# A vision-tower layer on one core: ScalarE clears the hidden-value tile, token weights arrive in three parts, and all five engines run their calls in another order

## The chip, the cores and the metric

The program runs on one core of a Trainium2 chip. The metric is the device time of one execution in microseconds (us). The profile is one further execution, recorded by the hardware profiler. Engine names: PE is TensorE (PEld its weight loads), DVE VectorE, ACT ScalarE, POOL GpSimd, SP SyncE, which here only issues DMAs.

## What is computed

```python
def reference(x, ...):                       # x: 32 images, 3 x 96 x 96, float32
    p = patches(x)                           # 32 x 36 tokens of 768 values
    h = layernorm(layernorm(p, ln1) @ W_tok, ln2)          # tokens of 192 values
    q, k, v = split(h @ W_qkv)               # 8 heads of 24 channels
    q, k = q / norm(q, tokens), k / norm(k, tokens)
    a = softmax(einsum('bnhd,bnhe->bhde', q, k) * temp)    # channel by channel, per image
    h = layernorm(h + (a applied to v) @ W_proj + b_proj)
    xn, sp = l2(h), l2(slots) * scale        # 8 experts of 4 slots
    logits = xn @ sp
    D, C = softmax(logits, experts), softmax(logits, all slots)
    H = gelu(down(einsum(xn, D)) + b_down)   # 24 hidden values per slot
    return layernorm(h + einsum(up(H) + b_up, C))
```

## The kernel before, in words

The 1152 tokens are handled in two cuts. For the token embedding there are 9 tiles `t` of 128 tokens; from attention on there are 11 groups `g` of up to 3 images, 108 tokens each (the last has 72). Everything is float32, and PE runs each float32 product as two matmul records.

Each engine runs its own list of calls, written out in the kernel; a call issues one to some dozens of instructions, and starts when semaphores say that its inputs are there and its output buffer is free. Each engine takes its list strictly in that order. So the order of the lists is the whole schedule.

Start: SP loads `gb1` (gain and offset of the first norm), the token weights `wt` (6 blocks of 128 x 192, in two DMAs), and the tokens twice, `xT` turned for the products and `xs` plain for the statistics. `first_products` (L449) multiplies a constant tile `still` 6 times, with a result that nobody reads. `column_means` and `offset` (L454, L464) multiply the weights by gain shares and by offsets; DVE makes the centred weights `wc` of them; `token(t)` (L473) is the embedding.

Per tile: `x_stats`, `x_moments` (DVE), `ln1_var`, `ln1_root` (POOL), `token_out` (DVE, reads the product), `token_stats`, `token_moments` (DVE), `ln2_var`, `ln2_root` (POOL), `ln2_norm` (DVE), `turn_h` (PE), `take_h` (ACT). `token(t)` may overwrite its PSUM bank only after `token_out(t-2)`. `keep_h_gain` and `keep_h_offset` (POOL) keep the normalised tokens for the residual. They need three rows that `load_rows` fetches and broadcasts to 128 partitions (`g2row`, `b2row`, `bprow`, one semaphore `rows_in` for all three). `regroup(g)` (SP) copies them to the layout by groups.

Per group, attention: `qkv` (PE), `square`, `take_qk`, `take_v`, `square_k` (ACT), `norms` and `gram` (PE), `norm_logs`, `norm_roots` (ACT), `q_scale` (POOL), `scales`, `scores`, `score_max`, `score_shift` (DVE), `exp_e` (ACT), `turn_p` (DVE), `mix` (PE), `y_sums`, `y_norm` (DVE), `project` (PE), `residual` and the norm after it. `qkv(g+1)` may overwrite only after `square(g)`, `take_qk(g)` and `take_v(g)`. `take_qk(0)` needs the small constant `imgsel`.

Per group, slots: `unit_h1` (DVE), `turn_xn`, `logits` (PE), `mask_logits` (DVE), `turn_l` (PE), the two softmaxes (`max_c`, `max_d`, `exp_c`, `exp_d`, `invert_sums`, `scale_d`), `turn_dc` and `slot_in` (PE). The experts run in two halves, groups 0 to 7 and 8 to 10: `hidden(b)` (PE), `gelu(b)` (ACT, after a table load), `spread(b)` (DVE) into `hb`, whose other places must be zero. Then per group `slot_out` (PE), `slot_bias` (DVE), `combine` (PE), `last_residual`, `last_stats`, `last_moments` (DVE), `ln4_root` (POOL), `last_shift` (DVE), `last_norm` (ACT) and `store` (SP). For the last group DVE ends it with `last_out`.

POOL clears tiles at the start; the last and largest is `hb`, L1202.

Of the kernel before, what the change touches and what calls it, by code (L numbers as in the profile page):

```python
# [74 lines left out]
def build(nc, x, x_t, w_tok, ln1_gb, ln2_g, ln2_b, g2col, b2col, w_qk, w_v, w_rest, w_proj, b_proj, temp, slots, scale,  # L75
# [3 lines left out]
    with ctx:  # L79
# [180 lines left out]
        wtok_in = [sem(f"wtok_in{i}") for i in range(2)]  # L260
# [187 lines left out]
        def _(pe):  # L448
            def first_products():  # L449
                pe.wait_ge(still_ready, 1)  # L450
                for _ in range(6):
                    pe.matmul(ps[:, 2, 0:D], still[:, 0:128], still[:, :], start=True, stop=True)

            def column_means():  # L454
                pe.wait_ge(gs1_ready, 1)
                for kc in range(KC):
                    if kc % (KC // 2) == 0:
                        pe.wait_ge(wtok_in[kc // (KC // 2)], 16)
# [4 lines left out]
            def offset():  # L463
                pe.wait_ge(ln1_in, 16)  # L464
                pe.wait_ge(wtok_in[0], 16)
                pe.wait_ge(wtok_in[1], 16)
# [218 lines left out]
            norms(5); turn_h(8); project(3); qkv(7); mix(4); norms(6); gram(5); turn_xn(0); project(4)
            logits(0); qkv(8); mix(5); norms(7); gram(6); turn_l(0); turn_xn(1); project(5); qkv(9)
            mix(6); gram(7); norms(8); logits(1); turn_dc(0); turn_xn(2); project(6); turn_l(1)
            norms(9); gram(8); qkv(10); gram(9); logits(2); turn_xn(3); mix(7); turn_l(2); slot_in(0)
            turn_xn(4); norms(10); logits(3); project(7); turn_dc(1); turn_l(3); logits(4); turn_xn(5)
# [662 lines left out]
```

## Time and profile before

| | us |
|---|---|
| median of 3 runs (112.24 to 112.75) | 112.63 |
| the profiled execution | 112.18 |
| its span, first to last instruction | 110.4 |

The profile's page gives, for the span of 110.4 us, each engine's busy time, the busy share in 40 slices, the chain of work that ended last, and groups of instructions. A PE that is busy throughout a stretch has no hole there; the ends of matmuls are modelled, so that does not say it works at its peak. The granted clock of the span is 0.991. A `[0.30 <-DVE h L757]` behind a row is the idle time of that engine before the instruction and what ended it.

### The profile page before, as it was taken

To read this page: it belongs to the slowest core of one execution; us is meant where nothing else is said; L and a number is where in the kernel's file an instruction comes from. 1 tells how busy PE (TensorE), PEld (TensorE's weight loads), DVE (VectorE), ACT (ScalarE), POOL (GpSimd) and SP (SyncE) were. 2 spreads that over 40 slices of the span, in tenths; PEclk is the share of its full clock that TensorE was granted. 3 is DMA by queue.
4 is the path that set the end of the run, shared out by engine and by line. 5 is a ranking of instruction groups with operands and counts; after the bars stand their busy time and mean duration, and the time that the engine had idled before them with its cause. 6 is when DMAs were issued, how large, how long until landed. Compare 5 with 4: busy or idle time off the path is not lost. (4 is left out here: it accounts for less than half of the span.)

```text
span 110.4 us, 4479 instructions
## 1 busy us (share of the span) xinstructions
PE 101.7 (92%) x1607; PEld 88.2 (80%) x1607; DVE 87.7 (79%) x380; ACT 67.5 (61%) x222; POOL 53.4 (48%) x126
## 2 busy tenths in 40 slices
PE   6999999999999999999999999799989989999900
PEld 6999989979999887887898887679779668879500
DVE  2129756968998958958977989999999897999960
ACT  4000023729563887798887996787785994476570
POOL 8800552263999887847204417906030340076880
PEclk9999999999999999999999999999999999999996
DMA  2999999469501111111000000010042000002232
GB/s 23 334 339 394 389 386 398 153 212 342 235 0 30 36 32 40 29 35 32 6 3 6 0 6 0 6 48 24 30 105 72 7 0 3 0 6 84 66 112 58
DMA packets 8554, 11.27 MB, mean 102 GB/s; under 512 B 2358, under 2 KB 5878, under 8 KB 8534
## 3 DMA queue, kind: packets, MB, share of 16 engines
q1 hardware_dynamic: 8533, 11.00, 29.5%
q8 instruction: 13, 0.21, 0.8%
q14 instruction: 8, 0.06, 0.2%
HBM read 9.22 MB, written 0.88 MB: 92 GB/s over the span
## 5 line engine op out<-in xcount | busy, mean ns | idle before, releaser
L480 PE MATMUL ps<-wc,xT 128*128 128x192 f32 x108 | 19.1, 330 | 0.0
L480 PEld LDWEIGHTS ps<-wc,xT 128*128 128x128 f32 x108 | 17.4, 190 | 0.7 <-issue 0.6
L1046 ACT ACTIVATE hT<-ps,b,g 128x128 f32<-128x128 f32 x18 | 7.3, 463 | 16.4 <-PE ps L491 16.3
L1068 ACT ACTIVATE km<-ps,imgsel 108x192 f32<-108x192 f32 (+1 forms) x32 | 11.1, 420 | 3.7 <-PE ps L515 3.6
L1256 POOL TENSOR_SCALAR mv<-mv 108x1 f32<-108x1 f32 (+1 forms) x11 | 3.0, 270 | 14.4 <-DVE mv L856 14.4
L568 PE MATMUL ps<-wp,yT 128*108 128x192 f32 (+1 forms) x44 | 9.3, 333 | 0.0
L664 PE MATMUL ps<-wu,hb 128*96 128x192 f32 (+1 forms) x44 | 9.2, 332 | 0.1
L1261 POOL TENSOR_TENSOR r<-mv,halves 108x2 f32<-108x2 f32 (+1 forms) x11 | 8.8, 803 | 0.8
L508 PE MATMUL ps<-wqk,hT 128*108 128x192 f32 (+1 forms) x44 | 9.0, 326 | 0.0
L726 DVE BATCH_NORM_STATS2 st<-xs 128x6 f32<-128x384 f32 x18 | 8.9, 537 | 0.0
L1249 POOL TENSOR_TENSOR rqt<-rn,tempc 128x6 f32<-128x6 f32 x11 | 2.2, 199 | 12.1 <-ACT rn L1105 12.1
L1207 POOL TENSOR_SCALAR var<-mv 128x1 f32<-128x1 f32 x9 | 2.0, 219 | 11.8 <-DVE mv L731 11.5
L1078 ACT ACTIVATE sqk<-km 108x576 f32<-108x576 f32 (+1 forms) x11 | 7.5, 683 | 0.0
L664 PEld LDWEIGHTS ps<-wu,hb 128*96 128x96 f32 (+1 forms) x44 | 6.5, 161 | 0.8 <-issue 0.4
L593 PE MATMUL ps<-sp,xnT 96*108 96x96 f32 (+1 forms) x44 | 6.2, 264 | 0.7 <-ACT xnT L1111 0.4
L568 PEld LDWEIGHTS ps<-wp,yT 128*108 128x108 f32 (+1 forms) x44 | 6.4, 170 | 0.5 <-DVE yT L836 0.2
L559 PE MATMUL ps<-vT,pc 32*32 32x37 f32 x512 | 6.8, 195 | 0.0
L1162 ACT ACTIVATE o<-z,sh,rstd 108x192 f32<-108x192 f32 x10 | 5.1, 543 | 2.8 <-DVE sh L980 2.8
L1269 POOL TENSOR_TENSOR rstd<-var,mhalf 108x1 f32<-108x1 f32 (+1 forms) x11 | 6.3, 576 | 0.9
L506 PE MATMUL ps<-hT,wv 128*128 128x108 f32 (+1 forms) x44 | 6.6, 273 | 0.0
L559 PEld LDWEIGHTS ps<-vT,pc 32*32 32x32 f32 x512 | 5.5, 104 | 1.3
L508 PEld LDWEIGHTS ps<-wqk,hT 128*108 128x108 f32 (+1 forms) x44 | 6.4, 171 | 0.0
(118 smaller groups left out, 296.6 us busy)
## 6 DMA issues: line engine op xcount, KB each, us to landing
xT<-in_x_t SPq DMA_DIRECT2D x9, 384.0 KB, 6.4
xs<-in_x SPq DMA_DIRECT2D x9, 384.0 KB, 6.2
out<-o SPq DMA_DIRECT2D x10, 81.0 KB
wt<-in_w_tok SPq DMA_DIRECT2D x2, 288.0 KB, 3.2
wqk<-in_w_qk SPq DMA_DIRECT2D x1, 192.0 KB, 5.9
wp<-in_w_proj SPq DMA_DIRECT2D x1, 192.0 KB, 10.0
wd<-in_w_down SPq DMA_DIRECT2D x1, 192.0 KB
z<-h SPq DMA_DIRECT2D x2, 81.0 KB
```

Source lines behind the costliest of these rows:

```text
L480: mm = pe.matmul(tokp(t), xT[:, o + kc * 128:o + (kc + 1) * 128], wc[:, kc, :], start=kc == 0, stop=kc == KC - 1)
L506: pe.matmul(vp(g)[:, m, :], wv[:, m, :], main, start=True, stop=False)
L508: pe.matmul(qkp(g)[:, m, :], main, wqk[:, m * D:(m + 1) * D], start=False, stop=False)
L559: mm = pe.matmul(yp(g)[r, m, i, :], pc[r, g % 2, GI * m + i, :], vT[r, m, g * GI + i, :], start=True, stop=True, tile_position=(32 * j, 32 ...
L568: mm = pe.matmul(prp(g), yT[:, g % NY, m, 0:images(g), :].rearrange("p i n -> p (i n)"), wp[:, m, :], start=m == 0, stop=m == 1)
L664: mm = pe.matmul(ytp(g), hb[:, e, i0:i0 + ni, :, :].rearrange("p i n q -> p (i n q)"), wu[:, e, :], start=e == 0, stop=e == 1)
L726: ins = dve.bn_stats(st1[:, t % 2, h, :], xs[:, t % NB, h * (PD // 2):(h + 1) * (PD // 2)])
L1046: ins = act.activation(hT[:, f, t * 128:(t + 1) * 128], htp(t)[:, f, :], ACT.Identity, bias=b2[:, f:f + 1], scale=g2[:, f:f + 1])
L1068: act.activation(km[0:n, g % NK, i, :], qkp(g)[:, 1, :], ACT.Copy, scale=imgsel[0:n, i:i + 1])
L1078: act.activation(sqk[0:n, g % 2, 0:ni, :], km[0:n, g % NK, 0:ni, :], ACT.Square).then_inc(sqk_ready, 1)
L1261: pool.tensor_tensor(r3[0:n, g, :], mv3[0:n, g, 1:3], halves[0:n, :], ALU.pow).then_inc(r3_ready, 1)
L1269: pool.tensor_tensor(rstd4[0:n, g:g + 1], var4[0:n, g:g + 1], mhalf[0:n, 0:1], ALU.pow).then_inc(rstd4_ready, 1)
```

## The change

`hb` is no longer cleared by POOL but by one ScalarE instruction, `clear_hidden`, with a semaphore of its own that only `spread(0)` waits for; the five clears that stay are counted with `cleared`, 5. The token weights come in `WP = 3` DMAs of two blocks each. `first_products` makes 5 products. All lists are written anew.

```diff
+WP = 3
-        wtok_in = [sem(f"wtok_in{i}") for i in range(2)]
+        wtok_in = [sem(f"wtok_in{i}") for i in range(WP)]
+        hb_cleared = sem("hb_cleared")
-                k0 = i * KC // 2
-                sp.dma_start(wt[:, k0:k0 + KC // 2, :].rearrange("p k e -> p (k e)"),
-                             w_tok[:, k0 * D:(k0 + KC // 2) * D]).then_inc(wtok_in[i], 16)
+                k0 = i * KC // WP
+                sp.dma_start(wt[:, k0:k0 + KC // WP, :].rearrange("p k e -> p (k e)"),
+                             w_tok[:, k0 * D:(k0 + KC // WP) * D]).then_inc(wtok_in[i], 16)
-                for _ in range(6):
+                for _ in range(5):
                     pe.matmul(ps[:, 2, 0:D], still[:, 0:128], still[:, :], start=True, stop=True)
-                    if kc % (KC // 2) == 0:
-                        pe.wait_ge(wtok_in[kc // (KC // 2)], 16)
+                    if kc % (KC // WP) == 0:
+                        pe.wait_ge(wtok_in[kc // (KC // WP)], 16)
-                    dve.wait_ge(cleared, 6)
+                    dve.wait_ge(hb_cleared, 1)
+            def clear_hidden():
+                act.wait_ge(still_ready, 1)
+                act.activation(hb[:, :, :, :, :].rearrange("p e i n q -> p (e i n q)"),
+                               still[:, 0:1].broadcast_to([128, 2 * B * NE * NP]), ACT.Copy,
+                               scale=0.0).then_inc(hb_cleared, 1)
-            take_h(0); take_h(1); square(0); take_qk(0); take_v(0); square_k(0); square(1); norm_logs(0)
+            take_h(0); take_h(1); square(0); take_qk(0); take_v(0); take_h(2); square_k(0); take_v(1)
+            take_qk(1); square(1); norm_logs(0); square_k(1); norm_roots(0); clear_hidden(); take_qk(2)
-            pool.memset(hb[:, :, :, :, :], 0.0).then_inc(cleared, 1)
-            pool.wait_ge(cleared, 6)
+            pool.wait_ge(cleared, 5)
-            ln2_root(1); ln1_var(2); ln1_root(2); ln2_var(2); ln1_var(3); ln2_root(2); ln1_root(3)
+            ln2_root(1); ln1_var(2); ln1_root(2); ln2_var(2); ln2_root(2); keep_h_gain(0); row_sum()
...
```

The new lists hold the same calls as the old ones, plus `load_token_weights(2)` and `clear_hidden()`.

SP, the DMAs of the first microseconds, with `load_rows` as `g2row`, `b2row`, `bprow`. Before:

```order
L395 DMA wrest<-in_w_rest 128x320
L375 DMA xT<-in_x_t 128x768
L390 DMA imgsel<-const_imgsel 128x3
L380 DMA xs<-in_x 128x768 x2
L375 DMA xT<-in_x_t 128x768 x2
L380 DMA xs<-in_x 128x768
L402 DMA g2row<-in_ln_g 128x192
L403 DMA b2row<-in_ln_b 128x192
L404 DMA bprow<-in_b_proj 128x192
L398 DMA tempc<-in_temp 128x2
```

and now:

```order
L397 DMA wrest<-in_w_rest 128x320
L377 DMA xT<-in_x_t 128x768
L404 DMA g2row<-in_ln_g 128x192
L405 DMA b2row<-in_ln_b 128x192
L406 DMA bprow<-in_b_proj 128x192
L392 DMA imgsel<-const_imgsel 128x3
L382 DMA xs<-in_x 128x768 x2
L409 DMA negmask<-const_negmask 128x96
```

The three rows have moved ahead of two `xT` and three `xs` tiles, and `imgsel` from in front of them to behind them.

POOL, after the root of the second norm of tile 1 (`mhalf` is the exponent of the root; `var1`, `rstd1` belong to the first norm, `var2`, `rstd2` to the second). Before:

```order
L1207 TENSOR_SCALAR var1<-mv1 128x1
L1211 TENSOR_TENSOR rstd1<-var1,mhalf 128x1
L1215 TENSOR_SCALAR var2<-mv2 128x1
L1207 TENSOR_SCALAR var1<-mv1 128x1
L1219 TENSOR_TENSOR rstd2<-var2,mhalf 128x1
L1211 TENSOR_TENSOR rstd1<-var1,mhalf 128x1
L1207 TENSOR_SCALAR var1<-mv1 128x1
L1211 TENSOR_TENSOR rstd1<-var1,mhalf 128x1
```

and now:

```order
L1214 TENSOR_SCALAR var1<-mv1 128x1
L1218 TENSOR_TENSOR rstd1<-var1,mhalf 128x1
L1222 TENSOR_SCALAR var2<-mv2 128x1
L1226 TENSOR_TENSOR rstd2<-var2,mhalf 128x1
L1233 TENSOR_TENSOR h0<-h0,g2row 128x192
L1243 TENSOR_TENSOR b2row<-b2row,bprow 128x192
L1233 TENSOR_TENSOR h0<-h0,g2row 128x192
L1214 TENSOR_SCALAR var1<-mv1 128x1
L1218 TENSOR_TENSOR rstd1<-var1,mhalf 128x1
```

`keep_h_gain(0)`, `row_sum` and `keep_h_gain(1)` now stand ahead of `ln1_var(3)`; before they stood behind `ln1_var(5)`.

PE, around `qkv(10)` (the first four lines of `hT,wv` to `hT,wrest`, 72 tokens) and `mix(7)` (`vT,pc`); `ident,lm` is `turn_l`, `sp3,xnT` is `logits`, `ident,xn` is `turn_xn`. Before:

```order
L515 MATMUL ps<-hT,wrest 128x72 x2
L545 MATMUL ps<-km,qp 32x72 x8
L593 MATMUL ps<-sp3,xnT 108x96 x2
L579 MATMUL ps<-ident,xn 96x108 x2
L559 MATMUL ps<-vT,pc 32x37 x24
L606 MATMUL ps<-ident,lm 96x108
L634 MATMUL ps<-dm,xn 96x96 x2
L579 MATMUL ps<-ident,xn 96x108 x2
```

and now:

```order
L595 MATMUL ps<-sp3,xnT 108x96 x2
L532 MATMUL ps<-imgsel,sq 32x3 x8
L536 MATMUL ps<-sqk,ones 32x144 x4
L547 MATMUL ps<-km,qp 32x72 x8
L608 MATMUL ps<-ident,lm 96x108
L508 MATMUL ps<-hT,wv 128x72 x2
L510 MATMUL ps<-wqk,hT 72x192 x2
L513 MATMUL ps<-wrest,hT 72x192 x2
L517 MATMUL ps<-hT,wrest 128x72 x2
L561 MATMUL ps<-vT,pc 32x37 x24
```

`logits(2)` and `turn_l(2)`, with more work between them, have moved ahead of `qkv(10)`; `mix(7)` still follows it.

## Rows read from the trace of the kernel before

**Rows 1.** The page: busy us, share, instructions; PE's busy tenths in 40 slices.

```profile
PE 101.7 (92%) x1607; PEld 88.2 (80%) x1607; DVE 87.7 (79%) x380; ACT 67.5 (61%) x222; POOL 53.4 (48%) x126
...
PE   6999999999999999999999999799989989999900
```

**Rows 2.** Stretches: us, each engine's busy (instructions), granted PE clock, DMA share, GB/s.

```profile
70.00:75.00 5.00, 4.19 (x100) 3.42 (x98) 5.00 (x27) 3.97 (x19) 1.89 (x4) 1.00 0.12 33
...
85.00:90.00 5.00, 4.36 (x87) 3.14 (x86) 4.59 (x22) 4.38 (x11) 1.75 (x4) 1.00 0.06 14
...
95.00:100.00 5.00, 4.68 (x61) 3.76 (x60) 4.75 (x25) 2.92 (x8) 2.79 (x8) 1.00 0.01 3
```

**Rows 3.** Timeline, PE, PEld and POOL at the start: start us, us, instruction, [idle before].

```profile
1.10 4.21 PE L452 MATMUL ps<-still 128*128 128x192 f32 x12 [1.10 <-DVE still L704]
3.17 1.85 POOL L1202 MEMSET hb<- 128x2048 f32 x1
5.10 2.54 PE L459 MATMUL ps<-wt,gs 128*128 128x192 f32 x12
7.48 2.11 PE L468 MATMUL ps<-wt,gb 128*128 128x192 f32 x12
11.33 0.22 POOL L1207 TENSOR_SCALAR var<-mv 128x1 f32<-128x1 f32 x1 [6.30 <-DVE mv L731]
15.45 0.20 PEld L491 LDWEIGHTS ps<-ident,h 128*128 128x128 f32 x2 [0.30 <-DVE h L757]
```

**Rows 4.** DMA issues: count, KB each, median us from issue to landing.

```profile
wt<-in_w_tok SPq DMA_DIRECT2D x2, 288.0 KB, 3.2
...
bprow<-in_b_proj SPq DMA_DIRECT2D x1, 96.0 KB, 10.4
...
tempc<-in_temp SPq DMA_DIRECT2D x1, 1.0 KB, 9.3
```

**Rows 5.** Timeline of SP's queue: issues behind which the constants land.

```profile
1.19 0.88 SPq L370 DMA_DIRECT2D wt<-in_w_tok  x2
...
13.46 0.43 SPq L404 DMA_DIRECT2D bprow<-in_b_proj  x1
13.94 0.43 SPq L398 DMA_DIRECT2D tempc<-in_temp  x1
```

**Rows 6.** Stretches as in rows 2, while the rows are fetched.

```profile
16.00:18.00 2.00, 2.00 (x16) 1.98 (x14) 1.52 (x4) 0.73 (x2) 0.44 (x1) 1.00 1.03 402
20.00:21.00 1.00, 1.00 (x7) 1.00 (x8) 1.00 (x4) 1.00 (x4) 0.00 (x0) 1.00 0.28 98
```

**Rows 7.** Timelines of PE, ACT and POOL, 18 to 28 us.

```profile
21.91 0.59 PE L506 MATMUL ps<-hT,wv 128*128 128x108 f32 x4
24.55 2.22 PE L480 MATMUL ps<-wc,xT 128*128 128x192 f32 x12
20.13 1.04 ACT L1068 ACTIVATE km<-ps,imgsel 108x192 f32<-108x192 f32 x3
21.25 0.38 ACT L1085 ACTIVATE vT<-ps 128x216 f32<-128x216 f32 x1
18.65 0.57 POOL L1211 TENSOR_TENSOR rstd<-var,mhalf 128x1 f32<-128x1 f32 x1
27.74 0.59 POOL L1236 TENSOR_TENSOR b2row<-b2row,bprow 128x192 f32<-128x192 f32 x1
```

**Rows 8.** ACT groups by shape: count, busy us, mean ns.

```profile
L1078 ACT ACTIVATE sqk<-km 108x576 f32<-108x576 f32 x10 | 7.0, 699 | 0.0
...
L1057 ACT ACTIVATE sq<-ps 108x192 f32<-108x192 f32 x10 | 3.4, 342 | 3.7 <-PE ps L515 3.7
```

**Rows 9.** Timeline: the longest hole on PE after the start.

```profile
71.47 0.30 PE L606 MATMUL ps<-ident,lm 108*96 108x108 f32 x1 [0.59 <-DVE lm L890]
```

**Rows 10.** Timelines of PE and DVE near the end.

```profile
99.58 0.58 PE L677 MATMUL ps<-yt,cT 96*108 96x192 f32 x2 [0.32 <-DVE yt L948]
107.39 0.37 DVE L974 TENSOR_SCALAR o<-z,mv,rstd 72x192 f32<-72x192 f32 x1 [0.69 <-POOL rstd L1269]
```

More of the change, by code:

```diff
@@ L464, in offset @@
                 pe.wait_ge(ln1_in, 16)
[L465 to L466 removed]
+                for i in range(WP):
+                    pe.wait_ge(wtok_in[i], 16)
                 for kc in range(KC):
@@ L685, in _ @@
[L685 to L689, printed above, removed]
@@ L690, in _ @@
-            mix(8); slot_in(1); turn_xn(6); turn_l(4); logits(5); turn_dc(2); project(8); turn_l(5)
-            logits(6); slot_in(2); gram(10); turn_l(6); turn_dc(3); turn_xn(7); mix(9); turn_dc(4)
+            token(3); turn_h(1); qkv(0); token(4); turn_h(2); qkv(1); norms(0); gram(0); token(5)
+            qkv(2); norms(1); turn_h(3); token(6); turn_h(4); qkv(3); norms(2); gram(1); mix(0)
+            token(7); project(0); turn_h(5); qkv(4); norms(3); gram(2); mix(1); token(8); project(1)
+            turn_h(6); qkv(5); mix(2); norms(4); gram(3); turn_h(7); project(2); qkv(6); mix(3)
@@ new lines, in _ @@
+            norms(5); gram(4); turn_h(8); project(3); qkv(7); mix(4); norms(6); gram(5); turn_xn(0)
+            project(4); logits(0); qkv(8); mix(5); gram(6); norms(7); turn_l(0); turn_xn(1); project(5)
+            qkv(9); gram(7); mix(6); logits(1); norms(8); gram(8); turn_l(1); turn_xn(2); project(6)
+            turn_xn(3); turn_dc(0); logits(2); norms(9); gram(9); turn_l(2); qkv(10); mix(7); turn_xn(4)
+            logits(3); slot_in(0); project(7); turn_l(3); turn_xn(5); turn_dc(1); logits(4); norms(10)
@@ new lines, in _ @@
+            take_qk(1); square(1); norm_logs(0); square_k(1); norm_roots(0); clear_hidden(); take_qk(2)
+            take_v(2); take_h(3); norm_logs(1); square(2); square_k(2); norm_roots(1); exp_e(0)
+            take_qk(3); norm_logs(2); norm_roots(2); take_v(3); take_h(4); square_k(3); square(3)
+            exp_e(1); square(4); take_qk(4); norm_logs(3); norm_roots(3); square_k(4); take_v(4)
+            take_h(5); exp_e(2); take_h(6); square(5); take_qk(5); take_v(5); square_k(5); take_h(7)
@@ new lines, in _ @@
+            norm_logs(4); exp_e(3); norm_roots(4); take_qk(6); take_v(6); square(6); norm_logs(5)
+            norm_roots(5); square_k(6); exp_e(4); take_h(8); square(7); take_v(7); take_qk(7)
+            take_xn(0); norm_logs(6); square_k(7); exp_e(5); norm_roots(6); take_qk(8); take_v(8)
+            square(8); exp_c(0); norm_logs(7); exp_d(0); square_k(8); take_xn(1); exp_e(6)
+            norm_roots(7); take_qk(9); take_v(9); square_k(9); norm_logs(8); norm_roots(8); take_xn(2)
+            exp_d(1); square(9); exp_c(1); take_c(0); exp_e(7); norm_logs(9); norm_roots(9); exp_e(8)
@@ new lines, in _ @@
+            exp_d(2); exp_c(2); take_xn(3); take_v(10); square(10); take_qk(10); take_xn(4)
+            take_slots(0); square_k(10); take_xn(5); exp_d(3); take_c(1); exp_e(9); exp_c(3); exp_c(4)
+            take_slots(1); take_xn(6); exp_d(4); take_c(2); norm_logs(10); norm_roots(10); exp_c(5)
+            take_slots(2); exp_d(5); take_xn(7); take_c(3); exp_c(6); exp_d(6); take_c(4); take_slots(3)
+            take_c(5); take_slots(4); exp_c(7); exp_d(7); take_c(6); take_slots(5); take_xn(8)
```

188 lines of the change are left out of this document (85 added, 103 removed).

## Prediction

> **What bounds the kernel now.** I read the page's busy line first [rows 1]. PE is busy for 101.7 of 110.4 us, DVE for 87.7. So PE is the first candidate, and the question is where it has holes. The slices say that from its first product to slice 25, 69 us, it is full [rows 1]. The stretches of 5 us give the size of the holes behind that [rows 2]: 0.81 us in 70 to 75, 0.64 in 85 to 90, 0.32 in 95 to 100. In 70 to 75 DVE is busy for all 5.00 us, and the longest hole ends with the masked logits that DVE writes [rows 9]. So there are three parts. Up to 70 us PE's work sets the time and an order can only lose, unless it takes work off PE. From 70 to 100 us PE and DVE alternate. After 105 us a short chain runs over POOL's roots to DVE's last instruction at 107.39 [rows 10]. The holes in these stretches sum to 1.77 us, which is about all that a new order alone can win on PE; removed work comes on top.
>
> **The constant product.** The 6 products take 4.21 us [rows 3], 0.70 each by their busy time. The 6 products of `offset`, of the same shape, take 2.11 us, 0.35 each. The granted clock is shown as full in these stretches, but the durations say that the first products run at the lower of the two levels, 1.2 GHz, and that the clock rises in the first of `column_means` at 5.10. With one product fewer PE reaches `column_means` 0.70 us earlier, if the weights are there. If the clock rises at the same time as before, since PE has worked without a break from 1.10 us as it did, two more records of `column_means` run at the low level, and 0.35 us is left. Bounds: 0 if the weights hold it up or the clock rises later by as much, 0.70 if the clock does not follow the time but the number of products. I take 0.35.
>
> Are the weights there? The two DMAs start at 1.19 us and 0.4 later and land 3.2 us after issue [rows 4, 5], so the first landed at about 4.4, and PE could start at 5.10 minus the weight load, 4.8. Now PE is ready at 4.1. The first part is 192 KB instead of 288 KB; 96 KB at the 402 GB/s of rows 6 is 0.24 us, so it lands at about 4.15. That just fits. The third issue puts everything behind it about 0.45 us later, and PE needs the first turned tile only after `offset`, near 9 us. I cost it at nothing.
>
> **The first wait for `ln2_norm(0)`.** `turn_h(0)` waits 0.30 us as a weight load for DVE's `ln2_norm(0)` [rows 3]; of that about 0.1 is a hole on PE. The new DVE list puts `x_moments(1)` directly behind `x_stats(1)`, so the root for tile 1 is earlier, and with it `token_out(1)`. `token_moments(1)` slips in ahead of `ln2_norm(0)`, for less than that. I take 0.10, bounds 0 and 0.15.
>
> **Clearing `hb`.** On POOL it ended at 5.0 us [rows 3]. POOL has no other work until the first statistics of the tokens, about 11 us, so taking it away gives nothing; the only thing that waited for all six clears was the end of POOL's own start. On ACT it becomes an instruction of 2048 values. ACT squares 192 values in 342 ns and 576 in 699 [rows 8], so 0.93 ns a value, and 2048 values would take 2.07 us. It stands behind `norm_roots(0)` and ahead of `take_qk(2)`. By the list ACT is through with group 1 near 26.4 us, and PE ends `qkv(2)` near 28.3. The hole is about 1.9 us. So the clear makes `take_qk(2)` late by up to 0.2 us. Behind it are `take_v(2)`, `take_h(3)`, `norm_logs(1)` and `square(2)`, and PE waits for that last one in `qkv(3)`, with hardly any slack, since the new list has only `token(6)` and small calls between `qkv(2)` and `qkv(3)`. Bounds: 0 and 0.5; I take a loss of 0.10. The Trainium skill (ScalarE: Activation LUTs, What ACT_TABLE_LOAD costs) gives 186 ns and 0.833 ns a value for such an instruction, 1.89 us; by that it would just fit the hole and cost nothing. The rows here have a steeper slope.
>
> **The rows of the norm, and `imgsel`.** This is the edit I weigh most. `bprow` was issued at 13.46 and landed 10.4 us later, at 23.86; the tiny `tempc` behind it landed 9.3 us after 13.94, at 23.24 [rows 4, 5]. Meanwhile the DMA rate fell from 402 to 98 GB/s [rows 6]: the broadcast rows pass slowly and hold up what is behind them. Nobody waited, since the rows were used from 27.7 us on [rows 7]. Now the rows are issued ahead of five tiles of 384 KB, and `imgsel` is behind them. Their landing has two bounds. If the data ahead of them set it, 1920 KB less at 402 GB/s are 4.9 us, so 19.0 us. If the issue sets it, five issues fewer of 0.48 us are 2.4 us, so 21.5. `imgsel` comes, like `tempc`, 0.6 us earlier: 18.4 to 20.9.
>
> Two calls wait for them. ACT's `take_qk(0)` needs `imgsel`; from its start to the end of `take_v(0)` are 1.50 us [rows 7], and `qkv(1)` can't start before. `qkv(1)` began at 21.91; now `turn_h(2)`, 0.2 us, is ahead of it and 0.45 us are saved, so it is due at 21.66 and `imgsel` at 20.16. POOL's `keep_h_gain(0)` needs all three rows and now stands ahead of `ln1_var(3)`, on which `token_out(3)` hangs, and `token(5)` needs that for its bank. Three steps of 0.59, the sum 0.22, the root 0.57 and 0.37 for `token_out` with 0.3 for the hand-overs are 3.2 us; `token(5)`, at 24.55 before, is due at 24.3, so the rows at 21.1. With 19.0 both are in time by more than a microsecond. With 21.5 `imgsel` costs 0.75 us, and the rows nothing more, since `token(5)` has then slipped by as much. I take 0, since 98 GB/s for several microseconds in the row speaks for a transfer that was held up by its turn and not by its issue; 0.75 stays for the range.
>
> The Trainium skill has a rule against this part of the change (DMA: Bandwidth & Descriptors, Queues, rings and completion order): a DMA's semaphore write lands only after every earlier write of that DMA engine, so a tiny load behind big ones lands with them. The landing of `tempc` at 9.3 us for 1 KB agrees. It gives no other sum, but makes it unlikely that `imgsel` overtakes the rows.
>
> **The order after 45 us.** Set by set, PE's list is the same again at `mix(8)`, which began at 75.01. In between the slot chain is moved ahead: `turn_xn(3)`, `logits(2)` and `turn_l(2)` now stand ahead of `qkv(10)`, and DVE's `mask_logits(2)` has some ten calls fewer ahead of it. On DVE `h1` and `unit_h1` of groups 0 to 4 move 10 to 20 places forward, to where DVE, with 79% over the whole span, is not full. That attacks the hole of 0.59 in its cause. Against it, `turn_p(7)` is 13 calls later on DVE, and `mix(7)` waits for it. Bounds: all 0.81 goes, or as much is added. I take 0.4.
>
> In 85 to 90 the holes come from ACT's table load ahead of `gelu(0)` and the wait for `take_xn(9)` behind it. That part of the lists is unchanged, and so are the 0.64 us. Near the end `combine(5)` waited 0.32 us for `slot_bias(5)` [rows 10], which DVE now runs 8 calls earlier; `combine(0)` to `combine(2)` come earlier on PE, so the last norms start earlier on DVE and POOL; and `take_c(10)` no longer stands ahead of the second table load, 0.2 us. With about 0.3 for the earlier last norms that is 0.8 in reach. But DVE is nearly full there, 4.75 of 5.00 [rows 2], and its work is not less. I take 0.45; bounds minus 0.3 and 0.8.
>
> **The sum.** 0.35 + 0.10 - 0.10 + 0.40 + 0.45 = 1.20 us. The span goes from 110.4 to 109.2, the profiled execution from 112.18 to 110.98. The median of the runs is 0.45 above that execution, so I expect the median at 112.63 - 1.20 = 111.4.
>
> **The rivals.**
> *Only the product counts.* PE saves its 0.45 at the start, and the moved calls win as many holes as they make. For it: no row shows that the planned order is met, and DVE, full from 70 to 80, has the same work. Against it: the hole at 71.47 has one plain cause and that is moved away. The time is 112.63 - 0.45 = 112.2. Chance 0.22.
> *The rows hold up the start.* `imgsel` and the rows land as late as they did, at 23.2 and 23.9, because what is slow is the broadcast itself and not its turn, and the tiles around it share its queues. Then `qkv(1)` is late by 23.24 - 20.16 = 3.1 us, PE's first hole, in the part where nothing is won back. The time is 111.4 + 3.1 = 114.5. It decides against the kernel before once `imgsel` lands after 21.4 us, 1.2 us past its due time. Against it: both bounds above are earlier. Chance 0.12.
> *The middle goes wrong.* `turn_p(7)` and other attention calls that are late on DVE double the hole of 0.81, the lower bound above. For it: 13 calls. 112.63 - 0.45 + 0.81 = 113.0. Chance 0.08.
> *More than I take.* The hole of 0.81 goes, the end gives its 0.8 and the clear costs nothing: with the 0.45 of the start 2.06 us, 110.6. Chance 0.13.
> My forecast has the rest, 0.45.
>
> **Range and chances.** The low end takes in the last rival and the high end leaves out the slow start and little else: 110.4 to 113.1. What can be told from no change here is about 0.5%, 0.56 us, so faster means below 112.07. The forecast and the good rival give 0.55 of their 0.58 to faster, the product alone 0.08 of its 0.22. Faster 0.63, same 0.20, slower 0.17.
>
> **What would show it.** The first product of `column_means` at 4.4 to 4.5 us and of `offset` at 7.1. No wait of ACT's `km` at 19.7 us for a DMA, and none of POOL for `g2row` past 21 us. The clear at 26.4, 1.9 to 2.1 us long, with no idle PE at 31 us. PE busy for more than 4.5 of 70 to 75 us. `combine(5)` without a wait. The forecast is wrong if PE has a hole of more than 0.3 us before 60 us.

## The result, and the profile after

The changed kernel is slower: 112.77 us (median of 20 runs, 111.83 to 114.13) against 112.00 of the kernel before (20 runs beside it, 111.24 to 112.77). The ratio is 1.0053, 95% interval 1.0027 to 1.0079. Ratios leave out executions more than 1.5% above the fastest of the same kernel (three of these 20, and later the traced ones of e5 and e17), which the medians include; so this one is nearer to 1 than 112.77 / 112.00 is. I had forecast 111.4 us, from a base of 112.63 that was the median of only three runs; my 1.20 us of gain, taken off 112.00, would have been 110.8.

The profiled execution took 112.19 us, its span 110.3, against 112.18 and 110.4 before. Two single executions say "equal", twenty of each say 0.5% slower. So the two traces are read for where time moved, and the sizes come from the repeated runs.

The page and the stretches of the changed kernel, as in [rows 1, 2]:

```profile
PE 102.1 (93%) x1605; PEld 89.0 (81%) x1605; DVE 88.9 (81%) x380; ACT 69.2 (63%) x223; POOL 53.3 (48%) x125
...
PE   5999999999999999999999999999999899998900
```

```profile
15.00:20.00 5.00, 5.00 (x37) 4.41 (x36) 3.31 (x12) 1.65 (x5) 2.38 (x6) 1.00 0.85 163
70.00:75.00 5.00, 5.00 (x155) 4.54 (x152) 4.57 (x25) 4.27 (x18) 1.19 (x3) 1.00 0.03 7
85.00:90.00 5.00, 4.37 (x85) 3.32 (x85) 4.39 (x22) 4.60 (x11) 2.31 (x4) 1.00 0.01 3
95.00:100.00 5.00, 4.58 (x60) 3.80 (x58) 4.54 (x23) 3.60 (x9) 3.56 (x8) 1.00 0.01 3
```

The hole of 0.81 us in 70 to 75 is gone, the one in 85 to 90 has stayed, and 95 to 100 has a little more than before. PE has two records fewer and still 0.4 us more of busy time. The start shows part of it (0.13 us over `first_products` and `column_means` together), beside [rows 3]:

```profile
1.11 3.57 PE L454 MATMUL ps<-still 128*128 128x192 f32 x10 [1.11 <-DVE still L706]
4.47 3.31 PE L461 MATMUL ps<-wt,gs 128*128 128x192 f32 x12
7.62 2.11 PE L470 MATMUL ps<-wt,gb 128*128 128x192 f32 x12
10.18 1.02 DVE L728 BATCH_NORM_STATS2 st<-xs 128x6 f32<-128x384 f32 x2 [0.32 <-DMA xs<-in_x]
15.51 0.20 PEld L493 LDWEIGHTS ps<-ident,h 128*128 128x128 f32 x2 [0.23 <-DVE h L759]
```

`column_means` begins 0.63 us sooner, but its 12 records take 3.31 us instead of 2.54. By the distance between their starts, 0.32 us at first and 0.16 later, eight of them began at the lower level here and three before, and `offset` begins 0.14 us later than before. The fourth row is new: DVE waits for `x(0)`, which SP now loads behind `xT(1)`.

From 18 to 32 us, as in [rows 7, 8] (the first row is of POOL, the second of PE's weight loads, the others of ACT):

```profile
20.12 0.65 POOL L1233 TENSOR_TENSOR h<-h,g2row 128x192 f32<-128x192 f32 x1 [0.44 <-DMA bprow<-in_b_proj]
24.86 1.92 PEld L482 LDWEIGHTS ps<-wc,xT 128*128 128x128 f32 x12 [0.20 <-DMA xT<-in_x_t]
26.67 1.95 ACT L1155 ACTIVATE hb<-still 128x2048 f32<-128x2048 f32 x1
28.93 0.42 ACT L1070 ACTIVATE km<-ps,imgsel 108x192 f32<-108x192 f32 x1 [0.31 <-PE ps L517]
```

The clear takes 1.95 us, and behind it ACT still waits 0.31 us for PE: it costs nothing. POOL waits for the rows, and `token(5)` for its tile a little.

The end is where the new order loses. PE, beside [rows 10]; L651 is `hidden(1)`, L666 `slot_out`, L679 `combine`:

```profile
97.28 0.49 PE L651 MATMUL ps<-xt,wd 96*32 96x32 f32 x32
97.70 0.58 PE L679 MATMUL ps<-yt,cT 96*108 96x192 f32 x2
98.11 1.47 PE L666 MATMUL ps<-wu,hb 128*96 128x192 f32 x8
100.00 1.21 PE L679 MATMUL ps<-yt,cT 96*108 96x192 f32 x4 [0.43 <-DVE yt L950]
101.04 1.47 PE L666 MATMUL ps<-wu,hb 128*96 128x192 f32 x8
102.47 0.58 PE L679 MATMUL ps<-yt,cT 96*108 96x192 f32 x2
103.77 1.05 PE L679 MATMUL ps<-yt,cT 96*108 96x192 f32 x4
```

`hidden(1)` starts at 97.28, 0.68 us ahead of before (97.96 there). `combine(5)` has lost its wait of 0.32 us [rows 10]. Yet `combine(9)` starts at 103.77, before at 103.82: 6.49 us from `hidden(1)` to `combine(9)` where it was 5.86. All but 0.05 us of that lead is given back in 6 us. PE's weight loads tell at which calls:

```profile
100.00 0.26 PEld L679 LDWEIGHTS ps<-yt,cT 96*108 96x108 f32 x2 [0.75 <-DVE yt L950]
100.63 0.27 PEld L679 LDWEIGHTS ps<-yt,cT 96*108 96x108 f32 x2 [0.36 <-DVE yt L950]
102.46 0.27 PEld L679 LDWEIGHTS ps<-yt,cT 96*108 96x108 f32 x2 [0.28 <-DVE yt L950]
```

`combine(6)`, `combine(7)` and `combine(8)` each wait for their `slot_bias`. Before, only `combine(5)` did, 0.64 us as a weight load. DVE in the same stretch shows why (L957 `last_residual`, L937 `spread(1)`, L950 `slot_bias`, L982 `last_shift`):

```profile
98.90 0.38 DVE L957 SCALAR_TENSOR_TENSOR z<-ps,rC,z 108x192 f32<-108x192 f32 x1
99.20 0.48 DVE L937 TENSOR_TENSOR hb<-hd,own 128x128 f32<-128x128 f32 x2
99.60 0.35 DVE L950 TENSOR_TENSOR yt<-ps,bu 96x192 f32<-96x192 f32 x1
100.14 0.16 DVE L982 SCALAR_TENSOR_TENSOR sh<-mv,rstd 108x1 f32<-108x1 f32 x1 [0.20 <-POOL rstd L1276]
100.22 0.35 DVE L950 TENSOR_TENSOR yt<-ps,bu 96x192 f32<-96x192 f32 x1
```

The hidden values are ready at 98.75, but `last_residual(5)` stands ahead of `spread(1)`, so that starts at 99.20. Then `last_shift(3)` waits 0.20 us for a root of POOL, with `slot_bias(7)` behind it. And that root is slow in this order:

```profile
98.98 1.13 POOL L1276 TENSOR_TENSOR rstd<-var,mhalf 108x1 f32<-108x1 f32 x1
100.39 0.57 POOL L1276 TENSOR_TENSOR rstd<-var,mhalf 108x1 f32<-108x1 f32 x1
```

The same instruction takes 0.57 to 0.60 us at all other places of this stretch.

### The profile page after: what moved, and what is told of

It reads as the page before. It is cut to its first block, busy times and chain, and to the rows that moved or that the text cites. A ratio compares the mean times of both kernels' runs of the same rounds, so it can differ in the third digit from the quotient of the medians.

```text
span 110.3 us, 4477 instructions
## 1 busy us (share of the span) xinstructions
PE 102.1 (93%) x1605; PEld 89.0 (81%) x1605; DVE 88.9 (81%) x380; ACT 69.2 (63%) x223; POOL 53.3 (48%) x125
## 4 chain that ended last, share of the span: by engine, by line
PE 75%; DVE 10%; issue 5%; POOL 5%; POOLq 1%; ACT 0%; DVEq 0%
PE ps L482 17%; PE ps L510 6%; PE ps L666 5%; PE ps L570 5%; PE ps L513 5%; PE ps L561 4%; PE ps L508 4%; PE ps L454 3%; POOL rstd L1276 3%; PE ps L461 3%; PE ps L547 3%; PE ps L679 2%; PE ps L493 2%; PE ps L536 2%; PE ps L636 2%
## 5 line engine op out<-in xcount | busy, mean ns | idle before, releaser
L666 PE MATMUL ps<-wu,hb 128*96 128x192 f32 (+1 forms) x44 | 8.8, 330 | 0.2
L666 PEld LDWEIGHTS ps<-wu,hb 128*96 128x96 f32 (+1 forms) x44 | 6.7, 161 | 0.8 <-issue 0.4
L1276 POOL TENSOR_TENSOR rstd<-var,mhalf 108x1 f32<-108x1 f32 (+1 forms) x11 | 6.8, 620 | 0.9
L1256 POOL TENSOR_TENSOR rqt<-rn,tempc 128x6 f32<-128x6 f32 x11 | 2.7, 249 | 8.2 <-ACT rn L1107 8.1
L1059 ACT ACTIVATE sq<-ps 108x192 f32<-108x192 f32 (+1 forms) x11 | 3.7, 340 | 4.7 <-PE ps L517 4.7
```

The costliest lines, as they stand in the source:

```text
L666: mm = pe.matmul(ytp(g), hb[:, e, i0:i0 + ni, :, :].rearrange("p i n q -> p (i n q)"), wu[:, e, :], start=e == 0, stop=e == 1)
L1276: pool.tensor_tensor(rstd4[0:n, g:g + 1], var4[0:n, g:g + 1], mhalf[0:n, 0:1], ALU.pow).then_inc(rstd4_ready, 1)
```

## The experiments

I divided the program at marks that every trace shows: `offset`, the `token(3)` behind `turn_h(0)`, `hidden(0)`, `hidden(1)`, `combine(9)`. Differences of start times of PE, in us:

```
                          offset  token(3)  token(3) to  hidden(1) to
                          starts  starts    hidden(0)    combine(9)
before                     7.48    15.72      70.35        5.86
changed                    7.62    15.79      69.57        6.49
e4_after_again             7.30    15.58      70.29        6.49
e1_rows_late               6.26    15.32      70.28        6.50
e2_old_tail                6.45    15.77      69.91        5.86
e3_start_only              7.40    15.97      70.35        5.87
e6_rows_behind_x4          7.57    15.77      70.24        6.48
e7_rows_and_tail           7.37    15.47      69.73        5.87
e8_new_tail_on_before      6.85    15.08      70.34        6.49
e9_x0_first                6.99    15.14      70.26        5.87
e10_x0_late_on_before      8.04    16.28      70.34        5.86
e11_spread_first           7.32    15.72      69.49        6.10
e12_pe_in_turn             6.95    15.92      70.54        6.70
e13_old_loads_old_end      7.20    15.22      71.36        5.87
e14_rows_split             7.71    15.85      69.82        5.86
e15_six_products           6.64    15.62      70.26        6.49
e16_middle_only            7.77    15.79      69.81        5.87
e5_imgsel_first            7.50    16.56      69.79        6.49
e17_rows_and_tail_again    7.21    16.40      69.83        5.87
```

`hidden(0)` to `hidden(1)` is 11.88 to 11.93 in all. Two stretches are rigid: the old middle takes 70.34 or 70.35 in all four kernels that have it, and the end takes 5.86 or 5.87 in the old order and 6.48 to 6.50 in the new one (e11 and e12 change that order). The new middle is not: two traces of the changed kernel, the first and e4, differ by 0.72. `offset` swings by 1.8 us over all traces. For each run below I give the median, the ratio to the kernel before on the same chip, and its 95% interval.

**e4, the changed kernel once more.** No edit.

> The changed kernel itself, as the base of this comparison. If its loss is its own and not of one chip, its ratio to the kernel before is again 1.003 to 1.008. Its profile says which waits are there each time: the theory of late loads expects PE's token(5) to wait for a turned tile again, by 0.2 us or more, and DVE's x_stats for xs tiles; the theory of the end expects combine(6) to wait 0.4 us for slot_bias(6). The theory of the clock (the constant products give nothing, since the clock rises at its own time) expects the first of offset between 7.3 and 7.7 us.

113.14 us, ratio 1.0081 (1.0049 to 1.0113): slower again. Its middle took 70.29 us, 0.72 more than in the first trace of the same kernel:

```profile
20.48 0.59 POOL L1233 TENSOR_TENSOR h<-h,g2row 128x192 f32<-128x192 f32 x1 [1.00 <-DMA bprow<-in_b_proj]
20.80 1.05 ACT L1070 ACTIVATE km<-ps,imgsel 108x192 f32<-108x192 f32 x3 [0.71 <-DMA imgsel<-const_imgsel]
22.42 0.52 PEld L508 LDWEIGHTS ps<-hT,wv 128*128 128x128 f32 x4 [0.58 <-issue]
```

`imgsel` landed at 20.7 us instead of 20.1, and PE was 0.2 us earlier at `token(3)`; so ACT waits 0.71 us for `imgsel`, and `qkv(1)` is late.

**e1, the rows late.**

```diff
 SP:   loads in the order of before (weights still in 3 parts)
 POOL: ... ln1_root(5)
+      row_sum(); keep_h_gain(0); keep_h_gain(1); keep_h_offset(0)
```

> The changed kernel with SP's loads in the order of the kernel before (token weights in 3 parts), and POOL's row_sum, keep_h_gain(0), keep_h_gain(1), keep_h_offset(0) behind ln1_root(5). Theory of late loads: the broadcast rows ahead of five tiles starve the tiles, the waits for xs and xT tiles go, and the runs are 0.5 to 0.9 us shorter than the changed kernel's, with less spread from run to run. Theory of the end: the time stays within 0.2 us of the changed kernel's, since a gain at the start is given back behind gelu(1).

113.05 us, 1.0096 (1.0059 to 1.0133). A miss by my own edit: it delayed POOL's root for `ln2_norm(4)`, and PE's weight load waited 0.74 us for that at 31.59. It says nothing on the rows.

**e2, the old end.**

```diff
 PE:  logits(10)
-     combine(0); slot_out(3); turn_l(10); combine(1); ...
+     (the list of before from here on)
 DVE: slot_bias(1)
-     max_d(9); slot_bias(2); mask_logits(10); ...
+     (the list of before from here on)
```

> The changed kernel with the end of PE's and DVE's lists as before (PE from slot_out(3) on, DVE from max_d(9) on). Theory of the end: last_residual(5) ahead of spread(1), and last_shift(3) and (4), which wait for POOL's roots, ahead of slot_bias(7) and (8), gave back 0.7 us; so 0.4 to 0.8 us shorter than the changed kernel. Theory of late loads: the same as the changed kernel within 0.2 us.

112.34 us, 1.0003 (0.9973 to 1.0034), 0.80 us below e4 on the same chip. The new end costs about what the traces say, 0.63.

**e3, the start alone.**

```diff
 (the kernel before)
+WP = 3      -for _ in range(6)   +for _ in range(5)
```

> The kernel before with the token weights in 3 parts and 5 constant products, and nothing else. My prediction: 0.35 us shorter than before. Theory of the clock: between 0 and 0.1 us, since the clock rises at a time that PE's products do not set, and a product fewer only puts real ones at the lower level. That the extra DMA issue holds the loads up: 0.1 to 0.4 us longer.

112.33 us, 1.0015 (0.9993 to 1.0036). No gain from three parts and five products. The trace shows a price that I had put at nothing:

```profile
11.63 1.02 DVE L728 BATCH_NORM_STATS2 st<-xs 128x6 f32<-128x384 f32 x2 [0.56 <-DMA xs<-in_x]
15.70 0.44 PE L493 MATMUL ps<-ident,h 128*128 128x128 f32 x2 [0.34 <-DVE h L759]
```

DVE waits 0.56 us for `x(1)`, and PE 0.34 at `turn_h(0)`. In the four traces with the weights in two parts (before, e8, e10, e16) DVE never waits for it; in the five with three parts and `x(0)` ahead of `xT(1)` it waits 0.56 (e3), 0.61 (e1), 0.31 (e9), 0.29 (e14) and 0.03 (e13). What this costs at the median is not shown.

**e5, `imgsel` ahead of the rows; e6, the rows behind `x(4)` as well.**

```diff
 e5 SP:   -load_rows(); load_imgsel()    +load_imgsel(); load_rows()
 e6 SP:   load_imgsel(); load_x(3); load_x(4); +load_rows()
    POOL: ln1_root(4); +keep_h_gain(0); row_sum(); keep_h_gain(1)
```

> The changed kernel with the load of imgsel moved from behind the three broadcast rows to in front of them, and nothing else. Theory of the rows as I had it as a rival: ACT's take_qk(0) waited 0.5 to 0.7 us for imgsel in two of three profiles and made qkv(1) late; so that wait goes, qkv(1) starts at 22.1 or earlier, and the time falls by 0 to 0.5 us. If POOL's wait for the rows themselves (1.0 us) sets token(5), token(5) stays near 25.0 and the time moves by less than 0.2 us.

> As e5, and the rows behind xs tile 4, and POOL's keep_h_gain(0), row_sum, keep_h_gain(1) behind ln1_root(4) instead of ahead of ln1_var(3). Theory of the rows: DVE no longer waits 0.8 to 1.6 us for the xs tiles at 21 us, POOL not for bprow, token(5) starts at 24.4 to 24.6 instead of 25.2, and the time is 0.4 to 0.7 us below the changed kernel. Theory that only the end counts: within 0.2 us of it.

e5: 112.65 us, 1.0034 (0.9997 to 1.0070). e6: 112.65, 1.0047 (1.0015 to 1.0079). e6 has no wait for `imgsel` or rows any more, and is not told apart from the changed kernel. So the rows are not the main loss.

**e7, e6 with the old end; e17, the same once more.**

> e6 with the end of PE's and DVE's lists as in the kernel before. Both theories together: 0.8 us from the end and 0.5 us from the rows, so 1.3 us below the changed kernel and 0.4 us below the kernel before; that would be the gain of the middle part, freed of what hid it. If the rows are worth nothing: level with the kernel before, as the old end alone was.

> The kernel of e7 once more, beside e16 on one chip, for the size of what is left of the gain: if e7's 0.9985 was luck, 1.000 to 1.003; if real, 0.995 to 0.999. If the start of the changed kernel (three parts, 5 products, moved loads) is worth anything, it is faster than e16.

e7: 111.89 us, 0.9985 (0.9957 to 1.0014), 0.76 below e6 on the same chip: the end once more. e17: 112.09, 0.9965 (0.9932 to 0.9997). Together they hint at a small gain over before; e7 alone does not show one.

**e8, the new end on the kernel before.**

```diff
 (the kernel before)
 PE:  logits(10)      +(the changed kernel's list from here on)
 DVE: slot_bias(1)    +(the changed kernel's list from here on)
```

> The kernel before with nothing changed but the end of PE's and DVE's lists, which is that of the changed kernel from the same cut. Theory of the end: 0.5 to 0.8 us longer than before; from hidden(1) to the last combine 6.5 us instead of 5.9. If the end was slow in the changed kernel only for what came before it: within 0.2 us of before.

112.58 us, 1.0038 (1.0003 to 1.0073), 0.43 us by the ratio; 6.49 us for the stretch. The slow root is there too, 1.14 us at 99.03. The end loses by itself.

**e9, `x(0)` first; e10, `x(0)` late on the kernel before.**

```diff
 e9  (e7) SP:      -load_turned(1); load_x(0)    +load_x(0); load_turned(1)
 e10 (before) SP:  -load_x(0); load_ident(); load_turned(1)
                   +load_turned(1); load_x(0); load_ident()
```

> The kernel of e7 with x(0) loaded ahead of xT(1), the rest of its loads in the same order. Theory (token(3) starts when ln2_norm(0) is done, and that hangs on x(0), which the new order of loads puts behind xT(1)): VectorE's wait for xs at x_stats(0) is gone, token(3) starts 0.3 to 0.5 us sooner than in e7, and the time is 0.3 to 0.5 us below e7, 0.4 to 0.7 us below the kernel before. Rival (x(0) costs nothing, the start is set by turn_h's chain on TensorE or by the clock): the same as e7, a ratio near 0.9985 to the kernel before. Second rival (xT(1) is now late): TensorE waits for it at token(1), 0.2 us or more.

> The kernel before with one edit: xT(1) is loaded ahead of x(0). Theory of x(0): VectorE waits 0.3 us or more for xs at x_stats(0), the time is 0.2 to 0.5 us longer than before. Rival (x(0) is hidden anyway): within 0.1 to 0.2 us of before.

e9: 112.10 us, 1.0017 (0.9987 to 1.0048), not the gain I expected. e10: 112.17, 1.0022 (0.9994 to 1.0049), within my rival's bound. The traces say when `x(0)` matters. e9 and e12 begin `offset` at the same time, 6.99 and 6.95. First e9:

```profile
8.94 6.01 PE L483 MATMUL ps<-wc,xT 128*128 128x192 f32 x36
14.87 0.44 PE L494 MATMUL ps<-ident,h 128*128 128x128 f32 x2
15.14 1.14 PE L483 MATMUL ps<-wc,xT 128*128 128x192 f32 x6
```

and e12, with `x(0)` in its new place:

```profile
8.90 4.06 PE L482 MATMUL ps<-wc,xT 128*128 128x192 f32 x24
13.53 2.19 PE L482 MATMUL ps<-wc,xT 128*128 128x192 f32 x12 [0.57 <-DVE y L742]
15.65 0.44 PE L493 MATMUL ps<-ident,h 128*128 128x128 f32 x2
```

In e12 DVE waited 1.12 us for `x(0)` at 10.30, so `token_out(0)` was late, PE stood 0.57 us ahead of `token(2)`, and `token(3)` began 0.78 us later than in e9. The same holds in all ten traces that have DVE's new list and `x(0)` behind `xT(1)`: DVE waits for `x(0)`, by 0.25 to 1.46 us, and `token(3)` begins 5.60 to 5.62 us after `x(0)` has let DVE go, wherever `offset` began. In the first trace of the changed kernel that is little, 8.17 us from `offset` to `token(3)` against 8.02 in e13 and e16, which have `x(0)` in its old place. In e5 `offset` began at 7.50, DVE waited until 10.94, and it was 9.06. And what e9 won it lost again: DVE waited 1.3 us for `xs` and PE's weight load 0.4 us for `xT` at `token(5)`, so its middle took 70.26 us. An early start reaches the waits for the tiles sooner; the tiles do not land sooner for it.

**e11, `spread(1)` first; e12, PE in turn.** Both are the changed kernel with one edit to the end.

```diff
 e11 DVE: last_moments(4); -last_residual(5); spread(1); slot_bias(6); last_shift(3); slot_bias(7)
                           +spread(1); slot_bias(6); slot_bias(7); last_residual(5); last_shift(3)
 e12 PE:  hidden(1); -combine(5); slot_out(6); slot_out(7); combine(6); combine(7); ...
                     +slot_out(6); combine(5); slot_out(7); combine(6); slot_out(8); ...
```

> The changed kernel with one edit: in VectorE's order of the end spread(1), slot_bias(6) and slot_bias(7) stand ahead of last_residual(5) and last_shift(3). Theory A (VectorE's order of the end is what gives the 0.6 us back): hidden(1) to combine(9) takes 5.9 to 6.1 us instead of 6.49, 0.4 to 0.7 us shorter than the changed kernel. Theory B (TensorE's pairs of slot_out and combine are): no gain, within 0.2 us of the changed kernel.

> The changed kernel with one edit: TensorE's end behind hidden(1) has slot_out and combine in turn as in the kernel before, VectorE's order stays the new one. Theory B (TensorE's pairs give the 0.6 us back): hidden(1) to combine(9) is near 5.9 us, 0.4 to 0.7 us shorter than the changed kernel. Theory A (VectorE's order): within 0.2 us of the changed kernel.

e11: 6.10 us for the stretch, 0.39 of the 0.63 are back; e12: 6.70, worse. So DVE's order makes most of the loss, and PE's old turn does not help beside DVE's new order. DVE's whole old order beside PE's new one was not run, so PE's share of the rest is open. In e11:

```profile
98.74 0.46 DVE L937 TENSOR_TENSOR hb<-hd,own 128x128 f32<-128x128 f32 x2
99.12 0.69 DVE L950 TENSOR_TENSOR yt<-ps,bu 96x192 f32<-96x192 f32 x2
99.73 0.40 DVE L957 SCALAR_TENSOR_TENSOR z<-ps,rC,z 108x192 f32<-108x192 f32 x1
100.28 0.55 PE L679 MATMUL ps<-yt,cT 96*108 96x192 f32 x2 [0.18 <-DVE z L957]
```

`spread(1)` runs 1.62 us behind the start of `hidden(1)` (97.12) instead of 1.92, the two biases follow at once, and POOL's root takes 0.60 us. But `combine(7)` may overwrite its bank only after `last_residual(5)`, which is now behind the biases, and PE waits 0.18 us for it: a call that is moved out of the way can be needed itself. The medians show less: e11 112.67 us, 1.0056 (1.0023 to 1.0088), not told apart from the changed kernel's 1.0053; e12 113.28, 1.0113 (1.0066 to 1.0161). For e11 the 0.39 us rest on the trace alone. e12 is also the execution with the latest constants:

```profile
21.41 0.59 POOL L1233 TENSOR_TENSOR h<-h,g2row 128x192 f32<-128x192 f32 x1 [1.59 <-DMA bprow<-in_b_proj]
21.51 1.04 ACT L1070 ACTIVATE km<-ps,imgsel 108x192 f32<-108x192 f32 x3 [1.08 <-DMA imgsel<-const_imgsel]
23.16 0.67 PE L508 MATMUL ps<-hT,wv 128*128 128x108 f32 x4 [0.74 <-ACT vT L1087]
```

**e13, old loads and old end; e14, with POOL's row calls split.**

```diff
 e13 SP:   loads in the order of before (3 weight parts); PE, DVE: the end of before
     POOL: ln1_root(4); +keep_h_gain(0); row_sum(); keep_h_gain(1)
 e14 (e13) POOL: ln1_root(5); +row_sum(); keep_h_gain(0) ...
                 ln2_root(4); +keep_h_gain(1); keep_h_offset(0); keep_h_gain(2)
```

> The changed kernel with the loads in the order of before (x(0) ahead of xT(1), the rows and imgsel behind the tiles; weights still in three parts), POOL's keep_h_gain(0), row_sum and keep_h_gain(1) behind ln1_root(4), and the end of TensorE's and VectorE's lists as before. Theory (the middle is worth 0.6 us, the moved loads and the new end are what gave it back): TensorE has no wait for a DMA or for imgsel before 30 us, hidden(1) to combine(9) takes 5.9 us, and the time is 0.4 to 0.7 us below before. POOL may wait for the rows until 23.9 us, which would cost up to 0.5 of that. Rival (the middle is worth nothing on the median, or the tiles come late in the old order too): within 0.2 us of before, like e7.

> As e13, but POOL has row_sum and keep_h_gain(0) behind ln1_root(5) and keep_h_gain(1), keep_h_offset(0), keep_h_gain(2) behind ln2_root(4), so that it waits for no row. Theory: if POOL's wait for the rows is what is left, 0.2 to 0.5 us below e13; if POOL's idle 1.8 us before 25 us are needed, its calls come too late up to 37 us, TensorE waits for them, and it is slower than e13 by 0.3 us or more. Rival: the same as e13.

e13: 112.77 us, 1.0058 (1.0029 to 1.0088), slower where I expected a gain:

```profile
25.03 0.59 POOL L1236 TENSOR_TENSOR h<-h,g2row 128x192 f32<-128x192 f32 x1 [2.12 <-DMA bprow<-in_b_proj]
28.55 0.32 DVE L758 TENSOR_SCALAR h<-y,mv,rstd 128x64 f32<-128x64 f32 x1 [0.91 <-POOL rstd L1229]
29.21 0.44 PE L494 MATMUL ps<-ident,h 128*128 128x128 f32 x2 [0.48 <-DVE h L760]
```

I had allowed for a wait until 23.9; the rows let POOL go at 25.03, it stood 2.12 us, and its root, DVE's `ln2_norm` and PE followed: a middle of 71.36 us. That is what it costs when POOL's place for the rows comes ahead of their landing. Taken out of the way in e14, the middle is 69.82 and the time 112.21, 1.0009 (0.9974 to 1.0045): 0.5% less than e13, no gain over before.

**e15, six products.**

```diff
 (the changed kernel)  -for _ in range(5)   +for _ in range(6)
```

> The changed kernel with 6 constant products, as before. My prediction's term (a product fewer saves 0.35 us): 0.35 us slower than the changed kernel. Theory now (the start of token(3) is set by x(0) and ln2_norm(0), and the clock's rise varies more than a product is worth): within 0.2 us of the changed kernel.

112.63 us, 1.0072 (1.0034 to 1.0109), not told apart from the changed kernel (1.0053, and 1.0081 in e4). Its start:

```profile
1.10 3.75 PE L454 MATMUL ps<-still 128*128 128x192 f32 x12 [1.10 <-DVE still L706]
4.69 2.11 PE L461 MATMUL ps<-wt,gs 128*128 128x192 f32 x12
```

With a product more, `column_means` began 0.41 us earlier than in the kernel before, since the clock rose inside the constant products, and all its records ran at the upper level. Here `offset` started at 6.64, but `token(3)` only at 15.62, since DVE waited 1.11 us for `x(0)`.

**e16, the middle alone.**

```diff
 (e14)  -WP = 3  +WP = 2    -for _ in range(5)  +for _ in range(6)
 SP:    loads exactly as before
```

> e14 with the start of before as well (weights in two parts, 6 constant products, loads exactly as before): only the new middle and the clear on ScalarE are left of the change. Theory (the middle alone is worth what the profiles say, 0.5 to 0.8 us from token(3) to hidden(0)): that stretch takes 69.5 to 69.9 us instead of 70.35, hidden(1) to combine(9) 5.9, and the median is 0.3 to 0.7 us below before. Rival (gains seen in single profiles don't reach the median, since the moment at which TensorE's clock rises varies by more and the new order has less slack): within 0.2 us of before, like e14.

111.84 us, 0.9962 (0.9936 to 0.9989): faster than the kernel before and than the changed one. Beside it on the same chip e17, with the changed kernel's start and its rows moved back, has 0.9965. The middle takes 69.81 us and the end 5.87:

```profile
97.50 0.49 PE L651 MATMUL ps<-xt,wd 96*32 96x32 f32 x32
97.92 0.89 PE L666 MATMUL ps<-wu,hb 128*96 128x192 f32 x4
99.13 0.58 PE L679 MATMUL ps<-yt,cT 96*108 96x192 f32 x2 [0.32 <-DVE yt L950]
```

`combine(5)` has its wait of 0.32 us back, and this end is the faster one.

## Why the prediction was wrong, by its steps

**The balance.** The middle alone gives 0.43 us on the median (e16) and 0.54 in the trace. The new end takes 0.63 in every trace, 0.76 and 0.80 between medians of one chip (e6 and e7, e4 and e2). From e2 (1.0003) to e7 and e17 (0.9985, 0.9965) 0.2 to 0.4 us lie in the place of the rows and `imgsel`, within overlapping intervals. 0.63 + 0.3 - 0.43 is 0.5 us slower; 1.0053 is 0.6. The end is tried both ways: with it alone on the kernel before, e8 is slower, if barely outside its interval; without it, e2 and e7 are level with before and below e4 and e6. How the rest divides over rows, `x(0)` and the third part is not shown.

**The step that failed is the end.** I took +0.45 us, bounds -0.3 and 0.8; it is -0.63, beyond my own lower bound. I counted the wait of 0.32 us for `slot_bias(5)` as a gain once it went. It went, but the waits of `combine(6)` to `combine(8)` came in its place. The earlier last norms, my other term there, did not come either: POOL starts on them at 96.11 instead of 96.39, yet `hidden(1)` is 0.68 earlier, so measured from `hidden(1)` POOL starts 0.40 later than before. The last stretch is a chain from `gelu(1)` over `spread(1)` and the `slot_bias` calls to the `combine` calls. I had looked at what had moved forward, not at what now stood in front of that chain; one call, `last_residual(5)`, and one that waits for POOL, `last_shift(3)`, are most of it (e11). Part of the chain is only the list's: `slot_out(6)` and `slot_out(7)` belong to the first half of the experts and need no `spread(1)`; it is DVE's order that puts `slot_bias(6)` behind it, in both kernels. Moving the bias ahead was not tried.

**The constant product**, +0.35: nothing that can be measured. I had fixed the clock's rise by one trace. Read from the starts of PE's single records, 0.32 us apart before it and 0.16 after, it came at 4.1 us in e1 and at 7.1 in e10 and e14, with PE busy without a break from 1.10 in all of them. Until the rise a record takes twice as long, so each microsecond by which it is later costs PE half a microsecond, and `offset` started between 6.26 and 7.71 us with five products and between 6.64 and 8.04 with six; the gain of one product can't be told in that. The Trainium skill (TensorE: Matmul & The Clock Gate, What's actually happening) says that the moment of the rise varies by half a microsecond to either side between executions. Here it is 1.5 to either side. And what is won at `offset` does not pass on: in the new order of loads `x(0)` sets `token(3)` in every trace (e9). My sum had no term for the place of `x(0)`, and the third part of the weights, which it had at nothing, made DVE wait for `x(1)` in e3.

**The first wait for `ln2_norm(0)`**, +0.10: it went from 0.30 to 0.23 us of the weight load's idle time. Where no tile is late it is worth more: from `offset` to `token(3)` are 8.02 us in e13 and e16 and 8.22 to 8.24 in the three kernels with the old start (before, e8, e10), so 0.2 us, above my bound of 0.15.

**The clear**, -0.10: 1.95 us in a hole that was large enough, cost 0. My slope from the rows gave 2.07. The estimate from the figures of the Trainium skill (ScalarE: Activation LUTs, What ACT_TABLE_LOAD costs), 1.89, was the nearer one, by 0.06 against 0.12.

**The rows and `imgsel`**, 0: right in the first trace, wrong as a value over the runs. `imgsel` landed at 20.1 in it, between my 18.4 and 20.9, and at 20.7 and 21.4 in e4 and e12. I had a due time of 20.16, no slack, and bounds of which one was late; 0 was the best case and not the middle. The rival of 3.1 us was too strong; its mechanism is there, with waits of 0.58 us for PE's weight load in e4 and 0.74 for PE in e12. The rate in 15 to 20 us is down to 163 GB/s while the rows pass (379 before). `imgsel`, 1.5 KB, issued at 11.96, landed 8.2 us later, 0.2 behind `bprow`. That fits the rule I weighed (the Trainium skill, DMA: Bandwidth & Descriptors, Queues, rings and completion order), but I had read too much into it: in the trace of before `tempc`, issued behind `bprow`, landed at 23.24, 0.6 us ahead of it, so a small load can pass a row.

**The middle**, +0.40: right in cause and size, though my reading of DVE's list was loose (`h1(2)` and `h1(4)` move 3 and 1 places back, not forward). `turn_l(2)` no longer waits for `mask_logits(2)`, 70 to 75 is full, and the rival of `turn_p(7)` did not come. It measures 0.54 in e16's trace, 0.86 in e11's, 0.78 in the changed kernel's first and 0.06 in its second, where the waits for the constants fall into the same stretch.

**My marks.** 4.47 for `column_means`, no wait of `km` for a DMA, none of POOL past 21 us, the clear, no idle PE at 31 us, 5.00 in 70 to 75, `combine(5)` without a wait, no hole above 0.3 before 60: all met, `offset` (7.62 instead of 7.1) alone was not. The forecast still failed, because no mark asked for the time from `hidden(1)` to the last `combine`, and that the first trace met so many was in part luck: e4, the same kernel, has the wait of `km` and that of PE.

**Open.** e14 against e16 (1.0009 and 0.9962, on two chips) hints that three parts and five products cost something, and so does DVE's wait for `x(1)`. e3 alone does not show it at the median, the intervals overlap, and e17, with three parts and five products, is level with e16 on one chip.

## What to carry to other kernels

In the last microseconds, look for the one chain that ends the kernel and put nothing on its engine in front of it, whatever wait that would remove elsewhere; a wait that vanishes there is no gain unless the last mark comes earlier. But look, too, for who needs the call that you move away. Put marks into the traces and compare stretches between them: here a stretch whose loads are all in time repeats within 0.02 us over many kernels, while the start swings by 1.8 us and hides 0.5%. And a load that is exactly in time in one trace is late in others of the same kernel.

## What the runs showed of the hardware

- POOL's root of 108 values takes 0.57 to 0.61 us, but 1.13 to 1.22 once in every trace with DVE's new end (the changed kernel, e1, e4 to e6, e8, e12, e15): there it starts 0.2 to 0.3 us ahead of `spread(1)`. Where `spread(1)` starts just ahead of it (the old end, and e11), it takes 0.57 to 0.61. The cause was not tried.
- The same loads land up to 1.3 us apart between executions: `imgsel` at 20.1, 20.7 and 21.4 us (changed kernel, e4, e12).
- The clock level rises anywhere from inside the constant products (e1, 4.1 us) to behind the middle of `column_means` (e14, 7.1 us). The granted clock of 0 to 10 us reads 1.00 in e1, in e15 and in the changed kernel all the same; only the durations tell 1.2 from 2.4 GHz there.
